# Six idle TensorE products at the end of each slot of the fill, in a gated cross-attention block

## The reference

```
qk     = Q K^T,  Q = layernorm(x) Wq + bq,  K = ctx Wk + bk,  V = ctx Wv + bv
scores = qk / 4
feats  = mean(scores), mean of row maxima, mean over rows of var(softmax(scores))
t      = exp(clip(MLP(feats)))           # 3 -> 64 -> 64 -> 1, one value per batch and head
attn   = softmax(qk / (2 t)) V
x2     = x + tanh(g_xattn) * (attn Wo + bo)
out    = x2 + tanh(g_ffn) * FFN(layernorm(x2))   # weights in three levels, activations in 8 bits
```

## Time and profile before

| | |
|---|---|
| runs | 846.73 us median of 3 (844.67 to 847.49) |
| profiled execution | 848.01 us; span 846.2 us |
| granted TensorE clock, mean | 0.951 |
| busy share | PE 86%, PEld 58%, DVE 86%, ACT 83%, POOL 61% |

### The profile page before, as it was taken

One profiled execution on the slowest core, in us unless ns is written; L12 is line 12 of the kernel. 1 busy time (PEld: TensorE's weight loads), 2 busy tenths in 40 slices (PEclk: granted clock), 3 DMA queues, 4 the chain that ended last, 5 costly groups with the idle time before them and its releaser, 6 DMA issues.

```text
span 846.2 us, 21376 instructions
## 1 busy us (share of the span) xinstructions
PE 724.9 (86%) x7350; PEld 490.9 (58%) x7350; DVE 725.5 (86%) x1500; ACT 704.8 (83%) x1448; POOL 516.4 (61%) x984
## 2 busy tenths in 40 slices
PE   5746688989898999989898989898998887688896
PEld 4323455666666666666666666666665565344554
DVE  5569896989898988989898989898988958779996
ACT  1466688999989898998999999989899887678896
POOL 5638754766666666666676666666653235545664
PEclk9655898999999999999999999999999979999999
DMA  6996674565556554657655755647461122122222
GB/s 165 208 275 140 115 166 91 125 117 137 126 118 143 120 147 118 142 121 144 117 134 122 139 111 136 134 119 139 113 133 33 46 79 86 49 75 69 75 82 76
DMA packets 119320, 101.18 MB, mean 120 GB/s; under 512 B 27423, under 2 KB 115615, under 8 KB 119199
## 3 DMA queue, kind: packets, MB, share of 16 engines
q1 hardware_dynamic: 116510, 98.36, 51.5%
q10 hardware_dynamic: 2704, 1.47, 0.7%
HBM read 49.54 MB, written 12.85 MB: 74 GB/s over the span
## 4 chain that ended last, share of the span: by engine, by line
PE 41%; ACT 25%; DVE 18%; issue 9%; POOL 3%; DMA 2%; SPq 2%; ACTq 0%; DVEq 0%; POOLq 0%
ACT ex L1068 9%; PE p_m L1271 8%; PE p_o L1178 7%; ACT pt L1058 7%; PE p_s L1161 5%; DVE stats L809 4%; PE p_t L1199 4%; PE p_m L1244 4%; PE p_m L1254 3%; PE p_m L1260 2%; DVE kst L935 2%; DVE hmax L938 2%; DVE nm L828 2%; ACT L1058 2%; ACT L1077 2%
## 5 line engine op out<-in xcount | busy, mean ns | idle before, releaser
L809 DVE BATCH_NORM_STATS2 stats<-ex 112x6 f32<-112x375 f32 x512 | 252.8, 535 | 36.5 <-ACT ex L1068 35.9
L1068 ACT ACTIVATE ex<-p_s,nm 112x375 f32<-112x375 f32 x512 | 270.0, 597 | 9.6 <-DVE nm L828 9.5
L1058 ACT ACTIVATE pt<-p_t,ct 128x336 f32<-128x336 f32 x488 | 240.3, 554 | 44.0 <-PE p_t L1199 40.7
L828 DVE TENSOR_REDUCE nm<-p_s 112x2 f32<-112x750 f32 x256 | 236.0, 922 | 1.4 <-PE p_s L1161 1.4
L1161 PE MATMUL p_s<-kst,qst 96*112 96x375 bf16 x512 | 136.3, 350 | 31.3 <-ACT ex L1068 29.9
L1199 PE MATMUL p_t<-qst,kst 99*128 99x112 bf16 x1464 | 117.2, 214 | 11.2 <-ACT pt L1058 9.2
L1199 PEld LDWEIGHTS p_t<-qst,kst 99*128 99x128 bf16 x1464 | 94.0, 98 | 55.5 <-ACT pt L1058 18.0
L1254 PE MATMUL p_m<-wv_sb,ctxt 128*128 128x256 f32 (+1 forms) x384 | 108.8, 407 | 10.0 <-DVE va L762 6.4
L1271 PE MATMUL p_m<-ctxt,wk_sb 128*128 128x375 f32 x256 | 103.2, 528 | 5.1 <-DVE qf L775 3.4
L1178 PE MATMUL p_o<-pt,va 128*32 128x112 f32 (+1 forms) x3072 | 102.2, 266 | 0.8 <-ACT ex L1068 0.5
L1178 PEld LDWEIGHTS p_o<-pt,va 128*32 128x32 f32 (+1 forms) x3072 | 70.8, 111 | 36.6 <-issue 30.3
(11 more groups left out here) (174 smaller groups left out, 1247.3 us busy)
## 6 DMA issues: line engine op xcount, KB each, us to landing
kst<-kp SPq DMA_DIRECT2D x384, 93.8 KB, 3.5
ctxt<-ctxt_dram SPq DMA_DIRECT2D x32, 375.0 KB, 4.4
qbounce<-qp SPq DMA_DIRECT2D x32, 168.0 KB, 2.5
qst<-qbounce SPq DMA_DIRECT2D x32, 168.0 KB, 3.4
qst<-qbounce SPq DMA_DIRECT2D x32, 112.0 KB, 3.4
xm<-x_dram SPq DMA_DIRECT2D x32, 112.0 KB, 2.3
x_dram<-x SPq DMA_DIRECT2D x32, 112.0 KB, 2.0
xt<-x_dram SPq DMA_DIRECT2D x28, 128.0 KB, 3.0
```

Of the source, the lines that this page charges most:

```text
L809: last = nc.vector.bn_stats(stats[:, nb % RING, 2 * pb + i], ex[0:SQ, 2 * (t % 2) + i, :])
L828: nc.vector.tensor_reduce(nm[:, n % RING, 2 * p:2 * p + 2], p_s[t % 2][0:SQ, :, 0:SK], axis=AX.X, op=ALU.max, negate=True).then_inc(s_max, 1)
L1058: nc.scalar.activation(pt[:, (2 * r + i) % 8], st_home(r, i)[:, 0:KC * SQ].rearrange("k (c q) -> k c q", c=KC), ACT.Exp, scale=ct[:, nr % ...
L1068: last = nc.scalar.activation(ex[0:SQ, 2 * ((t - 1) % 2) + i, :], p_s[(t - 1) % 2][0:SQ, i, 0:SK], ACT.Exp, bias=nm[:, ne % RING, h:h + 1])
```

## The change

At the end of PE's list of every slot from -3 to 25, after the third product of the MLP and before the totals product, PE makes six products of the ones tile with itself into the first 128 columns of the bank `p_t[1]`. Nothing waits for them and nobody reads them; the bank's next writer is PE itself.

```diff
--- before.py
+++ after.py
@@ -35,7 +35,7 @@
 STACK = len(K_STACK) * DK
 MROW = STACK
 
-SLOTS = 8
+SLOTS, WARM = 8, 6
 RING = 4
 KRING = 6
 CRING = 6
@@ -1290,6 +1290,9 @@
                     pe.wait_ge(s_g2, n // 2)
                     mm(t_h3, w3b[:, :], hid2[:, :], start=True, stop=True).then_inc(s_h3, 1)
 
+                if -3 <= t < BACK:
+                    for _ in range(WARM):
+                        mm(p_t[1][:, 0:P], ones, ones, start=True, stop=True)
                 if t == TOT_AT:
                     pe.wait_ge(s_abs, 3)
                     pe.wait_ge(s_prp, PRP_ONES)
```

## The result

| | before | changed |
|---|---|---|
| median | 846.73 us (844.67 to 848.53, 7 runs) | 852.08 us (849.42 to 856.01, 7 runs) |
| ratio | | 1.0061 (95%: 1.0037 to 1.0085) |
| profiled execution | 848.01 us, span 846.2 | 852.08 us, span 850.3 |
| granted clock, mean | 0.951 | 0.976 |

The forecast was 847.2 us, with 843.5 to 850.5 as its range. The changed kernel lies above it. The clock came as hoped, and the time went up nonetheless.

The account below looks back on a forecast made before the run. DVE, ACT and POOL bound most of the fill, PE's low clock its end; 0.4 + 0 + 0.2 + 0.2 = +0.8 us against 848.01 us, taken as +0.5 on the median 846.73: 847.2 us, range 843.5 to 850.5.

Parts of the forecast that it names:

- What bounds, the clock, and the price of a product: Fill: DVE, ACT, POOL bound most pieces; clock high from about 33 to 70 us; six products 1.35 us high, 2.55 low.
- Step A: Slots -3 to -1: 18 products make slot 0 start 3.9 us late, ends 2.6 and 4.2.
- signs of being wrong: Slot 0 after 36 us, clock falling between 36 and 67, POOL's split before 74, or stage lengths after 105 us differing.
- Step B: Slots 0 to 12: K of slot 10 at 58.9, not 57.00 us; its copy +0.4 us, ends -0.85 to +0.75.
- Step C: Totals in slot 12: K 1.4 us shorter, six products ahead of the totals add 1.35 us; net nothing.
- It hides behind nothing: Remark on the totals of slot 12: without the faster K they would be 1.35 us late.
- Step D: Slots 13 to 20: clock may be lost at 70 us, DVE's maximum 0.2 us late; ends 0 and 0.5.
- Step E: Slots 21 to 26: second GELU 1.3 us late, faster K pays back; +0.2 us, ends -0.3 and +0.8.
- the third rival: Behind the MLP, slots 21 and 22: products run at the low clock, 2.3 us on ACT's chain, 849.5 us; chance 0.2.
- That the clock stays low: Rival for slots 0 to 12: PE needs 56 us there instead of 35, kernel takes 867 us; chance 0.05.
- Those for a gain: Two rivals: three faster K products save 4.2 us, 842.5 us, chance 0.14; all low time halved, 824 us, chance 0.01.
- The last step of the sum: After slot 27 nothing is changed, so a shift of the fill reaches the end whole.

Follow-up runs that it names:

- e1: Kernel before plus the idle products of slots -3 to -1 only (18 products); ratio 0.9996 to before, median 847.74 us.
- e5: Changed kernel with DVE's four scalings moved from slot 13 to slot 11; ratio 1.0016 to before, median 849.74 us.
- e13: Kernel before plus only the six products of slot 12, between K and the totals; ratio 1.0049 to before, median 850.27 us.
- e4: Changed kernel with slot 12's totals product ahead of that slot's six products; ratio 1.0001 to before, median 847.11 us.
- e7: e4 with idle products in slots -3 to 20 only; ratio 1.0003 to before, median 847.44 us.
- e12: The changed kernel, unaltered, timed again on another chip; ratio 1.0058 to before, median 851.65 us.
- e2: Kernel before plus the idle products of slots 0 to 20 only (126 products); ratio 1.0004 to before, median 847.94 us.

## Why the prediction was wrong

**What bounds, the clock, and the price of a product** were right: 1.34 us a batch (1.35 taken), 0.91 to 1.00 of the clock (some 1 expected). **Step A** gave 3.9 us for slot 0, measured 3.9. Of the signs of being wrong, "slot 0 later than 36 us" did come (36.71), but 1.6 us of that is the later start of the whole profile. **Step B** gave K of slot 10 1.9 us late, measured 1.5; its copy 0.4 late, measured 0.2 (61.73 - 24.84 against 59.91 - 23.20, the two below the scatter). e1 confirms that the late start is taken up.

**Step C failed.** "The six products ahead of the totals add 1.35: nothing" was right about the totals, +0.1 us. It priced PE's time up to the totals and stopped there, and put what follows at nothing. K's other consumer, POOL, was made 1.4 us early against the totals by the same edit (L498 starts 1.20 us behind them, 2.58 before), and with that its pieces came to lie on DVE's: +0.6 us by nm of slot 13, of which L846 shows 0.45, and +2.4 us at the three multiplications. Moving the multiplications away takes 2.2 us of it back in the trace (e5). In the runs it was 3.7 us when the six stand alone (e13), and 5 us back when they stand behind the totals (e4), both with the 1.35 us of the totals in them. "It hides behind nothing" should have led me to ask what is queued behind the totals on DVE, ACT and POOL, and what it meets there. The rows of POOL and DVE before lay open, with the third multiplication four times as long as the second.

The Trainium skill, "SBUF — State Buffer", section "SBUF: two separate sides", says that VectorE and GpSimd share one pair of SBUF ports under an exclusive lock, held for a whole instruction by whoever starts first, for VectorE operations in a two-port mode or with two SBUF inputs. The traces agree in part: instructions that meet a long one of the other engine end with it (the first and third multiplication with the clip and the rounding, one of before with L500, L846 with L496), and either side can lose (e4, e7). They don't fit in who keeps its time: POOL's conversion in e4 started 1.0 us ahead of DVE's first multiplication and was itself the one drawn out, to 1.32 us. They don't show the lock itself, nor which of the two kinds these DVE operations are.

**Step D** expected the clock lost at 70 us and 0.2 us for it; it was kept (batches of 1.34 us there). In e12, the same kernel, it was lost there for one batch (2.77 us), and the stretch of the table is 14.0 us in both, so it cost nothing. POOL "hides what comes between" was true, but POOL itself started 2.7 us late.

**Step E failed in size, and the third rival took place.** I had +0.2 us with the clock kept and 2.3 more with the clock lost behind the MLP, at a chance of 0.2. Measured against the one profile of before: +0.35 with it kept, +1.65 to +2.24 with it lost. It was lost in one of the two profiles of the changed kernel and in three of the four that also have slot 20's products. So a chance of 0.2 was likely too low; the mechanism was right: the six products of slot 20 end well before the MLP's input, and those of slot 21, meant to bridge the wait, stood behind it.

**The other rivals.** That the clock stays low fell by the granted clock (0.91 to 1.00). Those for a gain fell by the result, and e1 and e2 bring none either: a K product does take 1.26 and not 2.66 us, but the products around it take about as much. By 0.91, 1.00 and 0.94 of the clock, some 39 of the 45.8 us at the low level were won, and no time with them. By the rule of the Trainium skill, "TensorE: Matmul & The Clock Gate", section "HAM oscillation — how this bites in real kernels", throttled time times one minus the clock ratio, that would have been near 20 us, by estimate. The runs differ: they show none of it.

**The last step of the sum**, that a shift of the fill is handed on to the end whole, isn't shown by the two profiles (5.0 us at slot 28, 2.4 at the end) and fits the medians (5.35 us).

## What to carry to other kernels

Ask of a delay on one queue not only who waits for it, but who does not: an engine that is fed from ahead of the delay gains on the others, and what it does next may meet their work where no semaphore keeps them apart. Look for pairs of DVE and POOL instructions on SBUF that end within a few hundredths of a microsecond of each other, and for small ones that take several times as long as their likes: a meeting that is cheap now can become dear when either engine moves. Fill an engine's wait from the front: idle products belong ahead of the instruction that waits. Behind it they found the clock lost in five of six profiles here, and delayed what the wait held up.

## What the runs showed of the hardware

- Three DVE multiplications of 128x64 fp32 in SBUF take 3.8 us when POOL's clip of 128x2048 fp32 (1.9 us) starts first and its rounding follows; the clip takes 2.02 to 2.10 instead of 1.89. Ahead of the clip they take 1.4 us, of which 0.78 is one that ends with POOL's L500; the shortest takes 0.19 to 0.20 in all 16 profiles.
- POOL's conversion L498 (128x375, 0.52 us) takes 0.83 to 1.32 in the nine profiles in which it ends with DVE's first multiplication, though it started ahead of it.
- A product of two 128x128 fp32 tiles is two records, 0.112 us apart at the high level: six take 1.34 us.
- The K product of slot -6 starts anywhere from 22.8 to 25.0 us in 16 profiles of kernels that are the same up to there, and the stretch behind nm of the last slot takes 173.7 to 178.7 us: 2.2 and 5.0 us of a span that have nothing to do with an edit.
